# Row-interleaved copies of the q/k operand with one 96-row fetch, and a reordered set-up

## The reference, cut to what matters

```python
def _phi(x, omega):
    proj = jnp.einsum('bhtd,dm->bhtm', x, omega)
    norm_sq_half = 0.5 * jnp.sum(x * x, axis=-1, keepdims=True)
    return jnp.exp(proj - norm_sq_half) / math.sqrt(m)
qkv = x @ W_attn + b_attn            # q, k scaled by 1/sqrt(d_h)
phi_q, phi_k = _phi(q, omega), _phi(k, omega)
S = jnp.cumsum(phi_k[..., :, None] * v[..., None, :], axis=2)
Z = jnp.cumsum(phi_k, axis=2)
y = einsum(phi_q, S) / (einsum(phi_q, Z)[..., None] + EPS)
return y @ W_proj + b_proj
...
# behind it: a second layer norm, a router with top 2 of 4 experts, and an FFN of 1024
# with low-rank terms per expert: h = relu(base + lora); out = sum_e w_e (h @ Wo)
h = _layernorm(x) * (1 + ca) + sa
x = x + ga * attention(h)
h = _layernorm(x) * (1 + cb) + sb
x = x + gb * ffn(h)
```

## Time and profile before

| | |
|---|---|
| median of three runs | 756.73 us (754.6 to 759.03) |
| profiled execution | 757.15 us, its span 754.8 us |
| PE busy | 733.7 us, 97% |
| DVE, ACT, POOL busy | 516.6, 428.1, 73.5 us |
| granted TensorE clock over the span | 0.995 |
| DMA traffic | 62.66 MB, 83 GB/s over the span |

### The profile page before, as it was taken

How to read it: one execution, slowest core, us unless ns; L and a number is a source line. 1 busy time by engine, 2 the same in 40 slices (tenths; PEclk the granted TensorE clock), 3 DMA queues, 4 the chain that set the end, 5 groups by cost and what they waited for, 6 DMA issues and landing times.

```text
span 754.8 us, 16910 instructions
## 1 busy us (share of the span) xinstructions
PE 733.7 (97%) x6080; PEld 592.9 (79%) x6080; DVE 516.6 (68%) x1254; ACT 428.1 (57%) x775; POOL 73.5 (10%) x82
## 2 busy tenths in 40 slices
PE   7899999999999999999999999999999999999797
PEld 4678769887788878887698877987788876888466
DVE  6547777577766776677766776757766777656566
ACT  5677455765566636665556655575456655665232
POOL 0560200002000110001000020000200010000200
PEclk9999999999999999999999999999999999999999
DMA  9850570106410273104701065101741028100000
GB/s 309 227 120 2 156 167 15 42 28 196 96 56 0 83 173 64 56 0 131 185 4 56 28 179 113 43 13 35 200 85 56 0 101 190 29 30 3 27 1 29
DMA packets 33929, 62.66 MB, mean 83 GB/s; under 512 B 3694, under 2 KB 17874, under 8 KB 33842
## 3 DMA queue, kind: packets, MB, share of 16 engines
q1 hardware_dynamic: 33334, 61.09, 30.3%
q10 hardware_dynamic: 576, 1.31, 0.5%
HBM read 40.37 MB, written 22.02 MB: 83 GB/s over the span
## 4 chain that ended last, share of the span: by engine, by line
PE 91%; DVE 3%; DMA 2%; ACT 1%; SPq 1%; issue 0%; POOL 0%; ACTq 0%; POOLq 0%; DVEq 0%
PE pa L546 13%; PE ring L679 12%; PE prod L559 8%; PE ring L525 6%; PE pa L421 5%; PE pa L422 5%; PE pa L423 5%; PE ring L579 4%; PE pa L666 4%; PE ring L530 3%; PE ring L768 2%; PE ring L586 2%; PE prod L546 2%; PE ring L701 2%; PE ring L760 2%; PE prod L525 2%
## 5 line engine op out<-in xcount | busy, mean ns | idle before, releaser
L1213 DVE TENSOR_TENSOR am_phk<-pa,const 128x512 f32<-128x512 f32 x112 | 77.0, 689 | 43.5 <-PE pa L546 42.8
L546 PE MATMUL pa<-phq,phkT 128*128 128x128 f32 x768 | 101.3, 275 | 0.0
L546 PEld LDWEIGHTS pa<-phq,phkT 128*128 128x128 f32 x768 | 95.3, 191 | 2.3 <-DVE am_phk L1213 0.2
L1393 DVE SCALAR_TENSOR_TENSOR am_phk<-ring,am_phk 128x512 f32<-128x512 f32 x64 | 44.1, 690 | 47.7 <-PE ring L768 47.7
L525 PE MATMUL ring<-xq,omega_x 100*128 100x512 f32 x198 | 71.1, 439 | 3.2 <-DMA xq<-norm_parts 2.2
L939 ACT ACTIVATE phq<-ring 128x512 f32<-128x512 f32 x84 | 50.6, 602 | 40.2 <-PE ring L525 39.2
L422 PE MATMUL pa<-wo_r,qk_l 128*128 128x256 f32 x248 | 69.7, 281 | 0.0
L421 PE MATMUL pa<-wo_r,qk_r 128*128 128x256 f32 x248 | 69.7, 281 | 0.0
L423 PE MATMUL pa<-wo_l,qk_r 128*128 128x256 f32 x248 | 69.6, 281 | 0.0
L1019 ACT ACTIVATE qk_r<-phq 128x512 fp32r<-128x512 f32 x64 | 40.5, 633 | 49.2 <-DVE phq L1399 49.2
L939 ACT ACTIVATE phkT<-ring 128x512 f32<-128x512 f32 x98 | 58.3, 595 | 13.3 <-PE ring L525 12.9
(11 more groups left out here) (208 smaller groups left out, 1616.1 us busy)
## 6 DMA issues: line engine op xcount, KB each, us to landing
xq<-qk_parts SPq DMA_DIRECT2D x45, 512.0 KB
qk_parts<-qk_r SPq DMA_DIRECT2D x32, 256.0 KB, 4.0
qk_parts<-qk_l SPq DMA_DIRECT2D x32, 256.0 KB, 4.6
xr<-in_L_attn_x SPq DMA_DIRECT2D x8, 512.0 KB, 3.4
out_x<-tg SPq DMA_DIRECT2D x16, 256.0 KB, 2.2
tok<-in_L_attn_x SPq DMA_DIRECT2D x7, 512.0 KB, 3.3
phq<-in_L_wmod SPq DMA_DIRECT2D x2, 512.0 KB, 7.2
am_phk<-in_wi_columns SPq DMA_DIRECT2D x2, 512.0 KB, 8.9
```

Of the source, the lines that this page charges most:

```text
L546: mm = pe.matmul(score_bank(q, a)[:, tt], phkT[:, q % 2, a, tt], query(q)[:, a, tt], start=True, stop=True)
L1213: dve.tensor_tensor(am[:, 2 * (q % 2) + a, :].rearrange("p (c t) -> p c t", c=NT), score_bank(q, a)[:].rearrange("p (c t) -> p c t", c=NT) ...
L1393: dve.scalar_tensor_tensor(r2[:, f % 2, :], z_bank[f % 4][:], 0.0, rho, ALU.max, ALU.mult).then_inc(r2_done.sem, 1)
```

## The change

The copies of the operand are interleaved row by row. `parts_out` has for each row of 128 three copies side by side (rounded, rounded, remainder), so the rounded part is sent twice and one DMA of 96 partitions fetches a half. Row 3r + c of `xq` is now row r of copy c; `omega_x` is laid out alike, and its remainder rows, no longer contiguous, are made on all 100 rows with a column of signs `om_sign` from the constants: two more DVE operations. The rounded part's sends wait for `sq_ready` (ACT's two evictions) and no longer for DVE's remainder.

In the set-up, SP sends the rounded norms before their remainder is ready, and sends parts 2 and 3 and half 1's norms before it fetches the second two pairs of half 0. TensorE makes q/k part 3 before the norms of half 0, and the second modulation's matmuls before the first feature tile. ACT and DVE split the two halves of wi apart, the second behind part 3, and move wo behind the norms of half 1.

```diff
-XROWS = 3 * PAIR_ROWS + 4
+COPIES = 3
+XROWS = COPIES * PAIR_ROWS + 4
...
-        qk_out = [sig(name, 4 * 16) for name in ("qk0_out", "qk1_out")]
+        qk_out = [sig(name, 2 * COPIES * 16) for name in ("qk0_out", "qk1_out")]
-        moved = [sig(name, 4 * 16) for name in ("moved0", "moved1")]
+        moved = [sig(name, 2 * 16) for name in ("moved0", "moved1")]
...
             def send(n, j):
-                wait(sp, qk_split, n, j + 1)
-                for part, src in enumerate((qk_r, qk_l)):
-                    sp.dma_start(parts_out[part, j // 2, :, j % 2], src[:, j, :].bitcast(F32)).then_inc(qk_out[j // 2].sem, 16)
-
-            def send_norms(n, half):
-                for part, src in enumerate((norm_r, norm_l)):
+                wait(sp, sq_ready, n, j + 1)
+                for copy, src in enumerate((qk_r, qk_r, qk_l)):
+                    if copy == 2:
+                        wait(sp, qk_split, n, j + 1)
+                    sp.dma_start(parts_out[j // 2, :, copy, j % 2], src[:, j, :].bitcast(F32)).then_inc(qk_out[j // 2].sem, 16)
+
+            def send_norms(n, half, parts=range(2)):
+                for part in parts:
+                    src = (norm_r, norm_l)[part]
...
             def fetch_qk(n, half, pairs, signal):
                 wait(sp, qk_out[half], n, qk_out[half].per)
-                for copy, part in enumerate((0, 0, 1)):
-                    src = parts_out[part, half].rearrange("(i r) k t -> r i (k t)", r=PAIR_ROWS)[:, pairs]
-                    sp.dma_start(xq[copy * PAIR_ROWS:(copy + 1) * PAIR_ROWS, half, pairs]
-                                 .rearrange("r i k t -> r i (k t)").bitcast(F32), src).then_inc(signal.sem, 16)
+                src = parts_out[half].rearrange("(i r) o k t -> (r o) i (k t)", r=PAIR_ROWS)[:, pairs]
+                sp.dma_start(xq[0:COPIES * PAIR_ROWS, half, pairs].rearrange("r i k t -> r i (k t)").bitcast(F32),
+                             src).then_inc(signal.sem, 16)
...
                 send(0, 0)
                 send(0, 1)
+                wait(sp, norm_full, 0, 1)
+                send_norms(0, 0, [0])
                 wait(sp, norm_split, 0, 1)
-                send_norms(0, 0)
+                send_norms(0, 0, [1])
                 fetch_qk(0, 0, one, lead_moved[0])
                 fetch_norms(0, 0, first, lead_moved[0])
                 fetch_qk(0, 0, two, lead_moved[1])
-                fetch_qk(0, 0, second, moved[0])
-                fetch_norms(0, 0, second, moved[0])
                 send(0, 2)
                 send(0, 3)
                 wait(sp, norm_split, 0, 2)
                 send_norms(0, 1)
+                fetch_qk(0, 0, second, moved[0])
+                fetch_norms(0, 0, second, moved[0])
                 fetch_qk(0, 1, both, moved[1])
                 fetch_norms(0, 1, both, moved[1])
...
             qk(0, 2)
+            qk(0, 3)
             norms(0, 0)
-            qk(0, 3)
...
             values(0)
-            features(0, 0, range(4), lead=True)
             pe.wait_ge(gates_sb.sem, 1)
             setup_mods(1)
-            features(0, 0, range(4, TILES), lead=True)
+            features(0, 0, range(TILES), lead=True)
...
-            setup_wi()
+            setup_wi([0])
             act.wait_ge(set_act.sem, 2)
             for j in range(3):
                 front_qk(0, j)
             front_norm(0, 0)
+            front_qk(0, 3)
+            setup_wi([1])
+            front_norm(0, 1)
+            setup_gate(0)
             act.wait_ge(ld_wo.sem, 16 * 2)
             setup_wo(0)
-            front_qk(0, 3)
-            setup_gate(0)
             setup_wo(1)
-            front_norm(0, 1)
...
             def setup_omega():
-                low = slice(PAIR_ROWS, 2 * PAIR_ROWS)
                 dve.wait_ge(ld_om.sem, 16)
                 dve.tensor_copy(omega_x[:], om_f).then_inc(om_high.sem, 1)
                 dve.wait_ge(om_high.sem, 1)
-                dve.tensor_tensor(omega_x[low, :], om_f[low, :], omega_x[low, :].bitcast(F32),
-                                  ALU.subtract).then_inc(om_done.sem, 1)
+                dve.wait_ge(ld_const.sem, 16)
+                dve.tensor_scalar(omega_x[:], omega_x[:].bitcast(F32), om_sign[0:XROWS, 0:1], None,
+                                  ALU.mult).then_inc(om_high.sem, 1)
+                dve.wait_ge(om_high.sem, 2)
+                dve.scalar_tensor_tensor(omega_x[:], om_f, om_sign[0:XROWS, 1:2], omega_x[:].bitcast(F32),
+                                         ALU.mult, ALU.add).then_inc(om_done.sem, 1)
...
-            setup_wi()
+            setup_wi([0])
             split_qk(0, 0)
             split_qk(0, 1)
             setup_omega()
             split_qk(0, 2)
             split_norm(0, 0)
+            split_qk(0, 3)
+            setup_wi([1])
+            split_norm(0, 1)
             setup_wo(0)
-            split_qk(0, 3)
-            setup_wo(1)
             dve.wait_ge(ld_vb.sem, 16)
-            values(0)
-            split_norm(0, 1)
+            values(0, [0])
+            setup_wo(1)
+            values(0, [1])
...
-    parts_out = nc.dram_tensor("qk_parts", (2, 2, P, 2, T), F32, kind="Internal").ap()
+    parts_out = nc.dram_tensor("qk_parts", (2, P, COPIES, 2, T), F32, kind="Internal").ap()
```

More of the change, by code:

```diff
@@ L85 @@
 F32R = mybir.dt.float32r
-CONSTS = {"ident": P, "causal": P, "headsum": VA, "prio": E, "expert": 2}
+CONSTS = {"ident": P, "causal": P, "headsum": VA, "prio": E, "expert": 2, "om_sign": 2}
 class Signal:
@@ L120, in build @@
             at += width
-        ident, causal, headsum, prio, expert = (cols[name] for name in CONSTS)
+        ident, causal, headsum, prio, expert, om_sign = (cols[name] for name in CONSTS)
         wa_r, wa_l = sb("wa_r", [P, KT, 3 * C], F32R), sb("wa_l", [P, KT, 3 * C], F32R)
@@ L343, in fetch_norms @@
                 src = norms_out[half, :, :, pairs].rearrange("q a i k t -> (q a) (i k t)")
-                sp.dma_start(xq[3 * PAIR_ROWS:XROWS, half, pairs].rearrange("r i k t -> r (i k t)").bitcast(F32),
+                sp.dma_start(xq[COPIES * PAIR_ROWS:XROWS, half, pairs].rearrange("r i k t -> r (i k t)").bitcast(F32),
                              src).then_inc(signal.sem, 16)
@@ L506, in features @@
                     if tile == 0 and lead:
-                        pe.wait_ge(lead_moved[0].sem, 4 * 16)
+                        pe.wait_ge(lead_moved[0].sem, 2 * 16)
                     if tile == TILES and lead:
-                        pe.wait_ge(lead_moved[1].sem, 3 * 16)
+                        pe.wait_ge(lead_moved[1].sem, 16)
                     if tile == 0 and not lead:
@@ L910, in front_norms, with setup_wi @@
                 act.activation(norm_r[:], norm_bank[1][:], ACT.Copy).then_inc(norm_full.sem, 2)
-            def setup_wi():
+            def setup_wi(ks):
                 act.wait_ge(ld_wi.sem, 16 * KT)
-                for k in range(KT):
+                for k in ks:
                     act.activation(wi_r[:, k, :], wi_raw[k], ACT.Copy).then_inc(late_act.sem, 1)
@@ L1452, in _ @@
             split_norm(0, 0)
+            split_qk(0, 3)
+            setup_wi([1])
+            split_norm(0, 1)
             setup_wo(0)
[L1454 removed]
+            dve.wait_ge(ld_vb.sem, 16)
+            values(0, [0])
             setup_wo(1)
[L1456 to L1458 removed]
+            values(0, [1])
             setup_lora()
@@ L1586, in constants @@
     expert = np.stack([r % 32 < LORA, r % 32 >= LORA], 1).astype(np.float32)
-    consts = np.concatenate([ident, causal, headsum, prio, expert], 1)
+    low_row = (r < COPIES * PAIR_ROWS) & (r % COPIES == 1)
+    om_sign = np.stack([np.where(low_row, -1, 1), low_row], 1).astype(np.float32)
+    consts = np.concatenate([ident, causal, headsum, prio, expert, om_sign], 1)
     rows = np.zeros((XROWS, 2 * M), np.float32)
@@ L1590, in constants @@
         for a in range(2):
-            rows[3 * PAIR_ROWS + 2 * part + a, a * M:(a + 1) * M] = -0.5
+            rows[COPIES * PAIR_ROWS + 2 * part + a, a * M:(a + 1) * M] = -0.5
     return {"consts": np.ascontiguousarray(consts), "norm_rows_padded": rows}
@@ L1602, in laid_out @@
     omega = rows['norm_rows_padded'].copy()
-    for k in range(3):
+    for copy in range(COPIES):
         for a in range(2):
-            omega[k * PAIR_ROWS + a * DH:k * PAIR_ROWS + (a + 1) * DH, a * M:(a + 1) * M] = rows['L0_attn_omega']
+            at = copy + COPIES * a * DH
+            omega[at:at + COPIES * DH:COPIES, a * M:(a + 1) * M] = rows['L0_attn_omega']
     return {
```

1 line of the change is left out of this document (removed).

## The result

The kernel after takes 760.43 us (median of 11 runs, 759.42 to 762.35), the kernel before on the same chip 757.12 (11 runs, 754.53 to 759.80). The ratio of the two, formed over the runs, is 1.0053 with an interval of 1.0037 to 1.0069: 0.5% slower, which is 4.0 us (2.8 to 5.2). The two medians alone are 3.3 us apart. The forecast was 757.6 within 753.0 to 762.0, and "no change" up to 760.5; both held, the second by 0.07 us. A small loss is there all the same, since the interval doesn't reach 1. The profiled execution of after took 759.42 us, span 757.1: it is the lowest of its runs, 1.0 under the median, so it shows 2.3 of the 4.0 us.

The account below looks back on a forecast made before the run. The prediction took TensorE, busy 97% of the span, to bound the kernel. Set-up -1.9 us and loop +2.8 us gave +0.9: 757.6 us by the median (forecast's chance 0.40), range of 8 in 10 from 753.0 to 762.0.

Parts of the forecast that it names:

- One fetch beside the norms' fetch: Loop: half 1's single fetch shares the norms' way into SBUF and delays them, 0.4 us a block, +2.8 us.
- rival (a): Loop: the entrance isn't shared enough to matter and the set-up gains 1.9 to 3 us; 754.5 us, chance 0.33.
- Rival (b): Loop: same sharing at full weight, tile 0 waits 0.9 us or more a block; 761 us and more, chance 0.17.
- Sends: Set-up: two more sends before the first fetch, 1.3 us on full engines; landing from 25.04 to 26.3.
- Fetch and first feature: Set-up: norms' fetch issued at 26.75 instead of 27.48, landing at 30.6 instead of 30.45; set-up term +0.1 us.
- Modulation ahead of the features: Set-up: the modulation's 2-column matmuls run in the gap after the values, -1.7 us.
- Clock: Set-up: the fall to 1.2 GHz comes again, now over the feature tiles, where 0.3 us less is lost; -0.3 us.
- Second fetch of half 0: Set-up: moved behind six sends and four of the norms, it lands at about 38.3, hidden from tile 12.
- Set-up in sum: Set-up: +0.1 - 1.7 - 0.3 = -1.9 us, bounds -3.2 to 0.
- Rival (c): Set-up: more bytes sent make the first fetch land at 31.5 to 32, set-up gain 0; 758.5 us, chance 0.10.
- The loop's sends and fetches cost nothing: Loop: third send per part and single 96-row fetch about balance; zero, with 0 to 0.2 us a block above it.

Follow-up runs that it names:

- wait_norms: Kernel after, but in the loop SP waits for half 0's norms to land before fetching half 1: 757.25 us, ratio 1.0005; run again 757.03 us, 1.0002.
- split_low: Kernel after, with half 1's fetch as two DMAs, rows 0 to 63 first, then 64 to 95: 758.09 us, ratio 1.0003.
- split_high: Kernel after, with half 1's fetch as two DMAs, rows 32 to 95 first, then 0 to 31: 758.40 us, ratio 1.0020.
- extra_send: Kernel after, with the rounded parts 0 and 1 of block 0 sent once more to memory nobody reads: 762.23 us, one run.
- setup_only: Kernel before, its layout and sends kept, with only after's set-up order on SP, PE, ACT and DVE: 756.99 us, ratio 0.9991.
- warm_gap: fetch_second_first plus two idle 512-column matmuls between the modulation and the first feature: 759.47 us, ratio 1.0031.
- row64_last: Kernel after, with half 1's fetch as three DMAs, rows 68 to 95, 0 to 63, then 64 to 67: 762.11 us, ratio 1.0062.
- fetch_second_first: wait_norms, with half 0's second two pairs fetched before parts 2 and 3 are sent in the set-up: 759.55 us, ratio 1.0024.
- third_pair: wait_norms, with pair 2 of half 0 fetched behind the lead and pair 3 behind the sends in the set-up: 756.26 us, ratio 0.9989.
- loads_later: third_pair, with the loads of low_t, bp_row, wp and bg_row issued behind pair 2's fetch: 756.61 us, ratio 1.0005.

## Why the prediction was right, and where not

- **One fetch beside the norms' fetch.** Right in place and sign, and mis-sized a little: 0.4 us a block forecast, 0.48 measured (0.40 of landing, 0.08 of later issue). The later issue was no part of the forecast; by the landing alone it was exact, and that is luck in part, since the 0.4 was a choice between 0 and 2.3. Waits of 0.43 to 1.04 us in all seven blocks, 0.3 to 0.6 forecast. wait_norms shows that the single fetch beside the norms is the cause, and the pair split_low/split_high that it is by its rows; rival (a) falls. What happens at the rows was not seen, only its effect on the landing. Rival (b) had the mechanism at 0.9 us a block, which isn't reached.
- **Sends.** Forecast +1.3 us on the landing; 26.44 - 25.04 = 1.4, and extra_send agrees. In the kernels with after's set-up order the landing lies at 25.9 to 26.8, with two sends (setup_only) at 25.6.
- **Fetch and first feature.** 30.6 forecast, 30.78 measured, from two errors that cancel: the norms' fetch was issued at 27.18 and not at 26.75, since SP waited for the norms' sends to land, and it landed 3.56 us later and not 3.87. Over the kernels the first feature lies between 29.5 and 32.2 (33.05 with the filler of warm_gap).
- **Modulation ahead of the features.** It happened, but of the 2 us at the scores only a part came: they start 1.0 us earlier in after. In the six executions with after's whole set-up order and loads (after, both of wait_norms, both splits, row64_last) they start between 31.97 and 34.35, so from 2.1 us earlier to 0.3 later than before.
- **Clock.** Forecast: the fall comes again, over the feature tiles, and costs 0.3 less. It came (0.59 and 0.55) over the scores as before: 16 matmuls took 3.25 us in both, so no 0.3 was won. And in some kernels there is a second fall behind the wait at tile 12 or 24, which the sum did not have. The price of a fall by itself isn't settled, since warm_gap was inconclusive.
- **Second fetch of half 0.** This step failed outright: "lands at about 38.3 ... Hidden". It landed at 40.50 (39.6 to 42.0 in the kernels with this order), and tile 12 waits 1.1 to 3.6 us. I had priced the six sends and the norms by their bytes, 3.9 us at 395 GB/s. The queue took 6.1 us (27.82 to 33.89) for the ten issues, and the transfer 6.2 us more, in a stretch where the DMA engines' share is 0.92 to 1.05. The cap on the gain that I put "near 3" came in after at 1.05 us: the scores behind tile 14 start at 41.45, before at 42.50.
- **Set-up in sum.** -1.9 forecast. From wait_norms (+0.4 and +0.2, loop as before), setup_only (-0.7) and after less its loop (+0.6 by the ratio, -0.1 by the medians) it is about 0. Rival (c) named this outcome for another reason: it let the first fetch land late, at 31.5 to 32, and in after it landed at 30.74 (in one kernel of this order, split_high, the first feature did start at 31.8).
- **The loop's sends and fetches cost nothing.** Right as far as the total can tell: wait_norms keeps them all and is at 1.0005 and 1.0002, with upper ends of the intervals at 1.7 and 1.1 us.

So +0.9 was forecast, +2.8 - 1.9, and +4.0 measured, +3.4 + 0.6. The loop's term carried the sign; the set-up's was the error of 2.5 us. That the total still lay in the range is owed to its width: 760.4 is nearer to the 761 of rival (b) than to the 757.6 of the forecast, and it got there without (b)'s 0.9 us a block. Behind the set-up's error stands more than one step: fetch_second_first, third_pair and loads_later each take one wait away, and it comes back as another wait or as a fall of the clock. The DMA engines are at a share near 1 for most of the stretch up to 46 us, and no order of the same bytes that I ran beat before; that the set-up stands at a limit there is my reading, not shown. How the loss divides between waits and clock stays open, as the set-up differs from one execution to the next: the first q/k matmul starts at 14.3 to 16.3 us whatever the kernel, and in the three executions that have exactly after's set-up (after and both of wait_norms) the loop begins at 103.4, 104.4 and 106.0 us. That is as much as the effects.

## What to carry to other kernels

A small transfer on which the bounding engine waits without slack should not be followed by a large one that writes into rows sharing its way in: choose the rows, or issue the large one when the small one has landed, which cost nothing here (1.0005 and 1.0002). Merging fetches saves SP issue time (1.26 to 0.32 us), and this is worth nothing unless SP is on the chain. When a fetch moves behind sends in a queue, price it by what issues and landings took in a stretch with the engines full, and not by bytes over the peak rate: here 6.1 us of issues and 6.2 of landing stood against the 3.9 that I had put. And one profiled execution can't price a set-up whose start moves by 2 us between executions.

## What the runs showed of the hardware

- One fetch of 96 rows is hardly faster per byte than three of 32. Half 1's fetch in block 1, windows of after:

```profile
105.00:107.00 2.00, 2.00 (x8) 1.25 (x8) 1.48 (x3) 1.58 (x3) 0.00 (x0) 1.00 1.05 227
107.00:109.00 2.00, 2.00 (x9) 1.32 (x8) 1.76 (x4) 1.93 (x4) 0.00 (x0) 1.00 0.98 221
```

  Before, the same two windows read 221 and 203. From the first issue to the end of the last recorded packet it is 9.4 to 9.9 us over the seven blocks, before 9.7 to 10.1; at 224 GB/s the 1.5 MB take 7.0 us of this. The prediction estimated 4.8 us for them, from the count of ports in the Trainium skill, "SBUF — State Buffer", section on door 1; here the estimate and the measurement differ, and the measurement decides. The 64-row fetch over both halves of SBUF did reach 424 GB/s. Why 96 rows don't isn't known; how the rows are dealt to the engines was not tried.
- Of the norms' fetch, its four recorded packets end at nearly the same time before and after (4.6 to 5.3 us behind the first send), and the semaphores come 0.4 us later. The delay doesn't show in the packets' own records; it sits between them and the semaphores.
- TensorE's clock falls to 1.2 GHz for 3.4 or 6.8 us after a stretch with little work, seen at about 12, 31, 40 and 50 us in one or the other kernel. A wait of 2.25 us at tile 24 (loads_later) was followed by a window at 0.50, the wait of 1.20 us at tile 12 of after was not (1.00 from 36 us on).
